# Experts stage of a two-layer metaformer kernel: when the next group's convolution, centring and gates are done

## The reference, cut to what matters

```python
def _L1_ffn_ref(x, router_w, router_b, expert_w, expert_b):
    router_probs = jax.nn.softmax(x @ router_w + router_b, axis=-1)
    top_p, top_i = jax.lax.top_k(router_probs, K)
    top_p = top_p / jnp.sum(top_p, axis=-1, keepdims=True)
    expert_out = jnp.einsum('bnd,edc->bnec', x, expert_w) + expert_b
    gathered = jnp.take_along_axis(expert_out, top_i[..., None], axis=2)
    return jnp.einsum('bnk,bnkc->bnc', top_p, gathered)

x = x + _L1_conv_ref(_ln_c(x), ...)      # 3x3 convolution, per-sample weights of low rank
t = _to_tokens(x)
t = t + _L1_ffn_ref(_ln_t(t), ...)       # _ln_t: mean and variance over the 128 channels
```

## Time and profile before

| | us |
|---|---|
| median of 3 runs | 2880.88 |
| lowest, highest | 2879.06, 2890.47 |
| the profiled execution | 2882.68 |
| its span (first to last instruction) | 2880.8 |
| in it, experts' loop, first matmul to the end | 2466.5 to 2880.8 |

### The profile page before, as it was taken

One profiled execution on the slowest core, in us unless ns is written; L12 is line 12 of the kernel. 1 busy time (PEld: TensorE's weight loads), 2 busy tenths in 40 slices (PEclk: granted clock), 3 DMA queues, 4 the chain that ended last, 5 costly groups with the idle time before them and its releaser, 6 DMA issues. The chain is left out here.

```text
span 2880.8 us, 78979 instructions
## 1 busy us (share of the span) xinstructions
PE 2343.8 (81%) x34528; PEld 1790.1 (62%) x34528; DVE 1492.2 (52%) x3491; ACT 1312.5 (46%) x2623; POOL 356.3 (12%) x682
## 2 busy tenths in 40 slices
PE   0455799958439999999999999999795984899898
PEld 0234788834128888888888888888532751344444
DVE  6342343447305565566666556666411453476777
ACT  0463243436215665566656666666310454333332
POOL 0112111114400000000000000000012001112221
PEclk9866798979769999999999999999998787899999
DMA  6436555536551111111111111100298520000000
GB/s 202 123 114 111 98 108 105 110 129 221 152 129 43 30 29 43 45 44 45 44 45 44 40 40 45 44 23 21 68 302 307 155 67 13 9 24 21 24 24 26
DMA packets 176948, 235.04 MB, mean 82 GB/s; under 512 B 32396, under 2 KB 134953, under 8 KB 173097
## 3 DMA queue, kind: packets, MB, share of 16 engines
q1 hardware_dynamic: 143749, 133.43, 16.7%
q0 software_dynamic: 32864, 96.64, 12.4%
HBM read 141.68 MB, written 88.31 MB: 80 GB/s over the span
## 5 line engine op out<-in xcount | busy, mean ns | idle before, releaser
L961 DVE COPY spc_g<-spc_pz 128x512 f32<-128x512 f32 x1024 | 629.5, 682 | 314.4 <-PE spc_pz L857 314.3
L931 ACT ACTIVATE spc_g<-spc_pz 128x512 f32<-128x512 f32 x1024 | 549.7, 610 | 291.6 <-PE spc_pz L857 291.1
L857 PE MATMUL spc_pz<-spc_v,spc_as 108*128 108x128 bf16 x8192 | 556.7, 220 | 20.5 <-issue 8.2
L857 PEld LDWEIGHTS spc_pz<-spc_v,spc_as 108*128 108x128 bf16 x8192 | 476.8, 98 | 108.9 <-ACT spc_g L931 31.4
L878 PE MATMUL spc_pz<-spc_g,spc_u 128*20 128x128 f32 x16384 | 467.0, 274 | 20.6 <-DVE spc_g L961 17.3
L878 PEld LDWEIGHTS spc_pz<-spc_g,spc_u 128*20 128x20 f32 x16384 | 451.0, 135 | 45.4 <-ACT spc_g L931 30.2
L1468 PE MATMUL moe_ex<-moe_ew,moe_d 128*128 128x512 f32 x512 | 250.2, 611 | 32.9 <-DVE moe_yt L1625 32.5
L842 PE MATMUL spc_pu<-spc_f,spc_s 128*128 128x256 f32 x768 | 208.6, 397 | 80.9 <-DMA spc_s<-s_sf 80.9
L1625 DVE SCALAR_TENSOR_TENSOR moe_yt<-moe_ex,moe_gb,moe_yt 128x128 f32<-128x128 f32 x768 | 209.6, 343 | 102.0 <-ACT moe_yt L1527 96.8
L501 DVE SCALAR_TENSOR_TENSOR inv_xo<-inv_pa,inv_mask,inv_xo 128x256 f32<-128x256 f32 x256 | 123.6, 484 | 222.5 <-PE inv_pa L459 162.1
L479 ACT ACTIVATE inv_b<-inv_pb 112x1024 f32<-112x1024 f32 x128 | 125.1, 1021 | 222.3 <-PE inv_pb L438 222.3
(11 more groups left out here) (205 smaller groups left out, 2251.2 us busy)
## 6 DMA issues: line engine op xcount, KB each, us to landing
s_yd<-spc_yo SPq DMA_DIRECT2D x128, 160.0 KB
s_sf<-fwd_so SPq DMA_DIRECT2D x16, 1024.0 KB, 6.5
spc_s<-s_sf POOLq DMA_DIRECT2D x32, 512.0 KB, 6.3
ivs_y<-s_yd POOLq DMA_DIRECT2D x32, 512.0 KB, 5.1
s_td<-ivs_to SPq DMA_DIRECT2D x32, 512.0 KB, 4.4
ln_t<-s_td SPq DMA_DIRECT2D x32, 512.0 KB, 3.8
inv_x<-s_xn SPq DMA_DIRECT2D x88, 112.0 KB
inv_x<-s_xn POOLq DMA_DIRECT2D x88, 112.0 KB, 7.9
```

The lines of the kernel that those rows point to most:

```text
L857: m = pe.matmul(pz[:, (p + 2) % 3, e // 4, 2 * FT * (e % 4):2 * FT * (e % 4) + 2 * FT], AS[:, x, 8 * p + e, :], V[:, k, x, :, FT * t:FT * ...
L931: act.activation(g_out(p, 0), g_in(p, 0), ACT.Copy).then_inc(ga, 1)
L961: v.tensor_copy(g_out(p, 1), g_in(p, 1)).then_inc(gd, 1)
```

## The change

It moves steps of the preparation between tiles of the same loop, and cuts two of the gate functions in two.

- `conv` and `add_conv` of chunk c are in tile c (c = 0 to 3), `centre` and `centred` of chunk c in tile c + 1. In a tile with both, `centre` of chunk t - 1 stands ahead of `conv` of chunk t.
- `scores` and `take_scores` are in tile 5, `turn_scores` and `spread` in 6, `softmax` in 8.
- `gate_argument` is in 7, `gate_probability` in 8; `gate_pick` is cut into 2 and 3 instructions, for tiles 9 and 10 and again (with `gate_without_first` ahead) for 11 and 12; `gate_weights` is cut into 4 and 2, for tiles 13 and 14.

All instructions, tiles and semaphores are the same.

```diff
                 if i + 1 < NGR:
-                    if t < 2 * GC and t % 2 == 0:
-                        conv(i + 1, t // 2)
-                    if t < 2 * GC and t % 2 == 1:
-                        centre(i + 1, t // 2)
-                    if t == 2 * GC:
+                    if 1 <= t <= GC:
+                        centre(i + 1, t - 1)
+                    if t < GC:
+                        conv(i + 1, t)
+                    if t == GC + 1:
                         scores(i + 1)
-                    if t == 2 * GC + 1:
+                    if t == GC + 2:
                         turn_scores(i + 1)
...
-                    if t < 2 * GC and t % 2 == 1:
-                        centred(i + 1, t // 2)
-                    if t == 2 * GC:
+                    if 1 <= t <= GC:
+                        centred(i + 1, t - 1)
+                    if t == GC + 1:
                         take_scores(i + 1)
-                    if t == 9:
+                    if t == GC + 2:
                         spread(i + 1)
-                    if t == 10:
+                    if t == GC + 4:
                         softmax(i + 1)
...
-            def gate_pick(i, src, col, hot):
+            def gate_pick(i, src, col, hot, part):
...
-            def gate_weights(i):
+            def gate_weights(i, part):
...
-                    if t < 2 * GC and t % 2 == 0:
-                        add_conv(i + 1, t // 2)
-                    if t == 10:
+                    if t < GC:
+                        add_conv(i + 1, t)
+                    if t == 7:
                         gate_argument(i + 1)
-                    if t == 11:
+                    if t == 8:
                         gate_probability(i + 1)
-                    if t == 12:
-                        gate_pick(i + 1, 3, 3, 6)
-                    if t == 13:
-                        gate_without_first(i + 1)
-                        gate_pick(i + 1, 4, 5, 5)
-                    if t == 14:
-                        gate_weights(i + 1)
+                    if t in (9, 10):
+                        gate_pick(i + 1, 3, 3, 6, t - 9)
+                    if t in (11, 12):
+                        if t == 11:
+                            gate_without_first(i + 1)
+                        gate_pick(i + 1, 4, 5, 5, t - 11)
+                    if t in (13, 14):
+                        gate_weights(i + 1, t - 13)
```

More of the change, by code:

```diff
@@ L1576, in gate_probability @@
                 step(v.tensor_tensor(g[:, 3], g[:, 2], bc(2), ALU.mult))
-            def gate_pick(i, src, col, hot):
+            def gate_pick(i, src, col, hot, part):
                 g = gb[:, i % 2]
[L1580 to L1584, removed]
+                if part == 0:
+                    step(v.tensor_reduce(g1[:, col], g[:, src], AX.X, ALU.max))
+                    step(v.tensor_tensor(g[:, 5], g[:, src], bc(col), ALU.is_equal))
+                else:
+                    step(v.tensor_tensor(g[:, 5], g[:, 5], row(prio), ALU.mult))
+                    step(v.tensor_reduce(g1[:, 4], g[:, 5], AX.X, ALU.max))
+                    step(v.tensor_tensor(g[:, hot], g[:, 5], bc(4), ALU.is_equal))
             def gate_without_first(i):
@@ L1588, in gate_without_first @@
                 step(v.scalar_tensor_tensor(g[:, 4], g[:, 6], -2.0, g[:, 3], ALU.mult, ALU.add))
-            def gate_weights(i):
+            def gate_weights(i, part):
                 g = gb[:, i % 2]
[L1592 to L1595, removed]
+                if part == 0:
+                    step(v.tensor_tensor(g1[:, 6], g1[:, 3], g1[:, 5], ALU.add))
+                    step(v.reciprocal(g1[:, 7], g1[:, 6]))
+                    step(v.tensor_tensor(g[:, 6], g[:, 6], g[:, 5], ALU.add))
+                    step(v.tensor_tensor(g[:, 6], g[:, 6], g[:, 3], ALU.mult))
+                    return
                 step(v.tensor_tensor(g[:, 7], g[:, 6], bc(7), ALU.mult))
@@ L1610, in _ @@
             gate_probability(0)
-            gate_pick(0, 3, 3, 6)
+            for part in range(2):
+                gate_pick(0, 3, 3, 6, part)
             gate_without_first(0)
-            gate_pick(0, 4, 5, 5)
-            gate_weights(0)
+            for part in range(2):
+                gate_pick(0, 4, 5, 5, part)
+            for part in range(2):
+                gate_weights(0, part)
             for idx in range(NTILE):
```

## The result

The change made the kernel slower. The median is 2932.13 us (2923.12 to 2935.04, 4 runs) against 2882.06 us for the kernel before, run beside it (4 runs); the ratio is 1.0162, 95% interval 1.0136 to 1.0189. The direction was as forecast; the size, 50 us, was more than twice the 20 us that were forecast, and the time lies outside the range.

A forecast was written before the change was run, and what follows sets the result against it. PE was taken as the early limit, DVE the late one: 33.44 + 20.85 = 54.29 us a group, 2.77 us more. Seven groups add 19.4 us, group 0 0.5 us: 2902.6 us profiled, 2901 us against the median; range 2891 to 2912 us.

The forecast's parts named there:

- The early pauses: Tiles 1 to 3: `conv` waits for ACT's copy and square, PE pausing 1.23 us each, 3.69 us a group.
- The late stretch: From tile 7's mixes to the next tile 0: DVE is the limit throughout, 20.85 us against 15.29 us before.
- ACT's wait ahead of softmax: Sign to look for in the profile after: ACT's 2.85 us wait ahead of `softmax` is gone.
- the 0.16 us taken off for them: Late stretch: the first pick's five steps shrink from 1.78 to 1.61 us without the collision with POOL's sum.
- The group at the full clock: Early and late stretch together: 33.44 + 20.85 = 54.29 us a group against 51.52 us before.
- The rival that the gates hide: Late tiles: gate pieces fit between the mixes, PE limits from tile 9, 50.26 us a group, 2872 us; chance 0.06.
- the check by tiles: Tiles 7 to 13: no gate piece fits the 0.60 us that a bare PE tile leaves DVE.
- the rival without a pause: Early tiles: `conv` need not stand still, 3.69 us go, 50.60 us a group, 2874 us; chance 0.06.
- The clock: Rival: PE's granted clock halves over the three paused tiles, giving 2990 us; chance 0.04.
- The low clock's price: Clock rival's cost: 4.28 us of PE work in each of three tiles takes up to twice as long, 12.8 us a group.
- Group 0: First group, partly at clock 0.71: 0.5 us added for a clock that comes back later, possibly some 2 us.

The follow-up runs named there:

- e1_fill: Changed kernel with two unused 128-row matmuls between `centre` and `conv` in tiles 1 to 3: 54.20 us a group, ratio 1.0058 to the kernel before.
- e7_fill9: Changed kernel with two unused matmuls over nine partitions between `centre` and `conv` in tiles 1 to 3: 58.13 us a group.
- e9_pad_long: Changed kernel with `conv` zero-padded to 128 partitions and two more ACT squares ahead of the one `conv` waits for: 57.93 us a group.
- e5_softmax: Kernel before with only `softmax` moved, from tile 10 to tile 11 behind that tile's activations: 50.72 us a group.
- e10_one_pause: Kernel before with one pause only, `conv` in tiles 0, 1, 3, 5 and `centre` in 1, 2, 4, 6, nine rows: 54.44 us a group.
- e2_pad: Changed kernel with `conv` padded with zeros from nine to 128 partitions, the pause kept: 53.23 us a group.

## Why the prediction was wrong

- **The early pauses: right.** `conv` 2.20 us behind `centre` (2.19 said), PE idle 1.18 us, 21 times; the tiles with a pause in which the clock held took 5.51 and 5.63 us.
- **The late stretch: right.** 20.72 us (20.85 said); ACT's wait ahead of softmax is not gone but fell from 2.85 us to 1.72 us, and behind it stood nothing that was late. No step of the picks ran into POOL's sum (0.28 and 0.29 us each), so the 0.16 us taken off for them came. The group at the full clock is 54.20 us (54.29 said), measured by e1_fill. The rival that the gates hide has fallen by this: not one piece fitted, as the check by tiles had it; the rival without a pause has too.
- **The clock: wrong, and it is the miss.** I had the mechanism among the rivals with 0.04. In groups 1 to 6 the falls cost 57.84 - 54.20 = 3.64 us each, 21.8 us, more than all that I forecast. The step that failed is the comparison that dismissed it: PE's idle 1.67 us in the earlier trace rows against a pause of 1.23 us. It compared idle times and left out what stood behind: behind the 1.67 us came 128-row experts, behind the pause the nine-row `conv`, which e7_fill9 shows to be no better than idle time. The row that named its nine rows, 9*128 9x512, was among.
- **The low clock's price** was overstated in the rival (12.8 us a group if all three tiles ran slow); the clock comes back within a tile, and each fall cost 1.69 us, two or three times a group.
- **Group 0: too low.** 0.5 us were put on top of the others' 2.77 us; it took 9.0 us. With the pauses filled group 0 took 66.87 us, 2.6 us less than the 69.48 us; with the padded `conv` the same layout costs 64.26 - 59.55 = 4.7 us there. PE starts this group at the low clock and comes up later; how the rest divides among its tiles I did not test.
- **Left out:** tile 1 of the last group, and all behind it, starts 1.0 us sooner.

The sum as it should have been: 6 x 2.69 + 9.0 - 1.0 + 21.8 = 45.9 us in the loop.

That the low clock is the default and activity lifts it is what the Trainium skill has, page "TensorE: Matmul & The Clock Gate", section "What's actually happening"; e9_pad_long agrees, with one fall of 1.7 us in each group behind 2.15 us of standing still. The prediction took idle time in the profile for the only lack of activity; e7_fill9, busy without a gap, shows that it is not.

What stays open: why two or three of a group's pauses bring a fall and not all, and how many rows between nine and 128 would do. Neither was tried. For the first there is a hint in e9_pad_long: from group to group the low stretch moves on by about 0.09 us against the tiles (tile 1 takes 7.32 us in group 1 and 6.88 us in group 6, tile 2 7.09 and 7.54 us), so where in a tile a fall begins is not set by the tile's own instructions alone.

## What to carry to other kernels

A step that waits for another engine straight behind its input puts the whole round trip on its engine's path (here 2.19 us between two starts, where 0.96 us would have done), even with 9% of that engine idle, and the round trip can be read beforehand wherever the same pair stands alone. Where a change puts such a wait on TensorE, look at what stands behind it: a matmul over nine partitions did no more to hold the clock than a gap of its length did, and here padding it with zeros to 128 partitions, or filling the gap with idle work over 128, cost no time and saved 4.6 and 3.6 us a group. Cutting work into smaller pieces hides only what fits into the spare time of a tile; moving one instruction behind the work it held up (softmax, 0.79 us a group in e5_softmax) was worth nearly as much as all the cutting and the earlier softmax together (0.97 us).

## What the runs showed of the hardware

- TensorE's granted clock fell to its lower level behind 1.18 us of idle time followed by a nine-row matmul of 1.05 us, behind nine-row matmuls of 2.3 us without idle time, behind a nine-row matmul and 0.85 us of idle time with half a tile's experts between, and behind 2.15 us of idle time. These did not bring it down every time: it fell behind 13 of 18 pauses in the kernel after and behind six of 18 in e9_pad_long, though behind all six in e10_one_pause. In all groups 1 to 6 it held behind 1.67 us of idle time and, three times a group, behind 1.2 us, where the matmuls behind had 128 rows (before, e2_pad). A fall cost 1.69 us.
- A `conv` over nine partitions cost more time than one over 128 with the same columns: padding the four of a group saved 1.22 us (51.51 to 50.29 us) at the same clock. In tile 6 it starts 0.32 us behind the second matmul of `final` and the next experts 1.05 us behind it, where padded these are 0.22 and 0.86 us.
- ScalarE's two table loads in `spread`, 1.28 us each, hold up the next tile's activations: in every kernel of the table DVE waits ahead of the mixes behind them (1.40 us before and in e10_one_pause, 1.99 us in the others).
